# Units of every tile read from x1 in SBUF instead of through a copy in DRAM

## What is computed

```python
e = stack([tbl_f[ids[:, f]] for f in range(24)], axis=1)          # (1024, 24, 16)
Xk = e
for W in (W0, W1, W2):                                             # 64 outputs each
    Wr = W.reshape(24, Xk.shape[1], 64)
    Xk = einsum('bfd,bhd,fho->bod', e, Xk, Wr)
    outs.append(Xk.sum(axis=2))
z = concatenate(outs, axis=1)                                      # (1024, 192)
h = relu(concatenate([z, dense_ctx], axis=1) @ W_top1 + b_top1)    # 512
h = relu(h @ W_top2 + b_top2)                                      # 256
y = h @ W_top3
```

## Time and profile before

| | us |
|---|---|
| median of 3 runs | 585.45 |
| lowest and highest | 584.02 and 591.72 |
| the profiled execution | 578.03 |
| its span in the profile | 576.2 |

### The profile page before, as it was taken

One profiled execution on the slowest core, in us unless ns is written; L12 is line 12 of the kernel. 1 busy time (PEld: TensorE's weight loads), 2 busy tenths in 40 slices (PEclk: granted clock), 3 DMA queues, 4 the chain that ended last, 5 costly groups with the idle time before them and its releaser, 6 DMA issues.

```text
span 576.2 us, 7709 instructions
## 1 busy us (share of the span) xinstructions
PE 370.3 (64%) x3000; PEld 168.8 (29%) x3000; DVE 307.3 (53%) x305; ACT 137.1 (24%) x282; POOL 187.3 (33%) x196
## 2 busy tenths in 40 slices
PE   0010200856088439726998269755999998999995
PEld 0010000212022115302452025212553553553554
DVE  1010001473278347643789348526799798798930
ACT  1000000001022113302333123303253353251253
POOL 6777773027506720672017700771000000000000
PEclk9999999977779759976999869777999999999999
DMA  6000100191436326721757246702756847848300
GB/s 163 6 7 7 7 7 4 41 252 29 98 107 150 86 60 190 211 57 40 190 165 188 45 123 186 197 7 63 227 160 173 222 139 195 221 140 208 90 1 1
DMA packets 28039, 64.30 MB, mean 112 GB/s; under 512 B 7311, under 2 KB 10823, under 8 KB 28012
## 3 DMA queue, kind: packets, MB, share of 16 engines
q1 hardware_dynamic: 21868, 62.35, 40.3%
q0 software_dynamic: 6144, 1.59, 3.0%
HBM read 53.86 MB, written 5.85 MB: 104 GB/s over the span
## 4 chain that ended last, share of the span: by engine, by line
another core or an unknown queue 33%; PE 24%; DMA 14%; DVE 11%; issue 8%; ACT 4%; POOL 4%; SPq 2%; DVEq 0%; ACTq 0%
PE acc L622 14%; DVE pairs L416 8%; DMA units<-x_dram 5%; DMA turned<-x_dram 5%; POOL emb L388 4%; PE spread L596 2%; DMA x_dram<-common 2%; PE misc L683 1%; ACT x0diag L489 1%; DVE z L421 1%; SPq L328 1%; ACT x0parts L476 1%; DVE rest L284 1%; DMA units<-x 1%
## 5 line engine op out<-in xcount | busy, mean ns | idle before, releaser
L416 DVE TENSOR_TENSOR pairs<-spread,units 128x1024 f32<-128x1024 f32 x192 | 225.9, 1218 | 118.3 <-remote 76.4
L388 POOL DMA_INDIRECT emb<-in_tbl,ids_sb x192 | 187.1, 975 | 203.2 <-DVE parts L288 143.6
L622 PE MATMUL acc<-pairs,w_sb 128*64 128x512 f32 x768 | 205.2, 642 | 4.4 <-DVE pairs L416 4.3
L596 PE MATMUL spread<-x0parts,sel 72*64 72x512 bf16 (+1 forms) x280 | 50.6, 450 | 116.9 <-ACT common L476 39.6
L622 PEld LDWEIGHTS acc<-pairs,w_sb 128*64 128x64 f32 x768 | 53.3, 146 | 76.0 <-issue 54.3
L416 DVE TENSOR_TENSOR pairs<-turned,common 120x1024 f32<-120x1024 f32 x42 | 51.1, 1220 | 24.6 <-DMA turned<-x_dram 24.6
L596 PEld LDWEIGHTS spread<-x0parts,sel 72*64 72x64 bf16 (+1 forms) x280 | 14.6, 121 | 159.3 <-ACT common L476 71.4
L643 PE MATMUL misc<-ident_b,parts 128*72 128x128 bf16 x120 | 11.7, 253 | 67.0 <-DVE parts L288 36.9
L622 PE MATMUL acc<-pairs,w 120*64 120x512 f32 x180 | 49.6, 636 | 2.4 <-DVE z L421 2.1
L416 DVE TENSOR_TENSOR pairs<-spread,common 120x1024 f32<-120x1024 f32 x6 | 7.3, 1223 | 68.9 <-remote 65.1
L476 ACT ACTIVATE x<-acc 128x512 f32<-128x512 f32 x31 | 18.7, 602 | 96.8 <-PE acc L622 80.2
(11 more groups left out here) (57 smaller groups left out, 192.6 us busy)
## 6 DMA issues: line engine op xcount, KB each, us to landing
units<-x_dram SPq DMA_DIRECT2D x56, 512.0 KB, 6.2
turned<-x_dram SPq DMA_DIRECT2D x42, 480.0 KB
units<-x SPq DMA_DIRECT2D x16, 256.0 KB, 5.1
x_dram<-x SPq DMA_DIRECT2D x28, 128.0 KB
emb<-in_tbl,ids_sb POOLq DMA_INDIRECT x192
x_dram<-common SPq DMA_DIRECT2D x14, 96.0 KB
x_dram<-common SPq DMA_DIRECT2D x14, 56.0 KB
w_sb<-in_w SPq DMA_DIRECT2D x2, 384.0 KB
```

Source lines behind the costliest of these rows:

```text
L388: pool.indirect_dma_start(out=e3[:, f, :], out_offset=None, in_=tables[f], in_offset=bass.IndirectOffsetOnAxis(ap=ids_sb[:, t, f:f + 1], a ...
L416: dve.tensor_tensor(pairs[buf][0:rows, :], source[0:rows, :], other[0:rows, h * HALF:(h + 1) * HALF], ALU.mult).then_inc(pairs_done, 1)
L596: last = pe.matmul(spread[ring][lo:hi, half * BLK:(half + 1) * BLK], sel[:, first + lo:first + hi], src[:, cols(h, half)], start=True, sto ...
L622: last = pe.matmul(acc[half * H:(half + 1) * H, :], w, pairs[buf][0:rows, half * BLK:(half + 1) * BLK], start=first, stop=final)
```

## The change

The DRAM copy of x1 goes, with `store_x1`, its semaphore and its waits. `load_units` now loads every tile as `first_units` loaded tile 0: two DMAs of 256 KB per j straight from `x1` in SBUF, after x1_done. SP's order becomes: units of (0, 0) and (0, 1); then for each t from 1 to 7 the x0 store and the three turned loads of (t, 0), the same of (t, 1), the units of (t, 0), the units of (t, 1). ACT's `x1_read` waits are taken out. DVE's wait for the units counts two DMAs per load. Nothing else of PE, DVE, ACT or POOL changes.

```diff
--- before.py
+++ after.py
@@ -182,7 +182,6 @@
             return spread[o // 2 % 2][:, o % 2 * BLK:(o % 2 + 1) * BLK]
 
         x0_dram = [nc.dram_tensor(f"x0_dram{h}", (X0_ROWS, HALF), F32).ap() for h in range(2)]
-        x1_dram = [nc.dram_tensor(f"x1_dram{h}", (H, HALF), F32).ap() for h in range(2)]
 
         spread = [ctx.enter_context(nc.psum_tensor(f"spread{s}", [P, HALF], F32)) for s in range(2)]
         acc2 = ctx.enter_context(nc.psum_tensor("acc2", [P, 2, BLK], F32))
@@ -205,7 +204,6 @@
         common_done = sem("common_done")
         x0_stored = sem("x0_stored")
         turned_in = [sem(f"turned_in{c}") for c in range(L1_CHUNKS)]
-        x1_stored = sem("x1_stored")
         units_in = [[[sem(f"units_in{s}_{h}_{j}") for j in range(UNIT_GROUPS)] for h in range(2)] for s in range(2)]
         pairs_done = sem("pairs_done")
         main_done = sem("main_done")
@@ -300,33 +298,18 @@
                              (bt1_sb[:, :], bt1), (bt2_sb[:, :], bt2), (dense[H:H + D, :], dense_t)):
                 sp.dma_start(dst, src).then_inc(mlp_in, 16)
 
-            def store_x1(t, h):
+            def load_units(t, h):
 
                 sp.wait_ge(x1_done, 2 * t + h + 1)
-                for half in range(2):
-                    sp.dma_start(x1_dram[h][:, half * BLK:(half + 1) * BLK], x1[half * H:(half + 1) * H, h, :])\
-                        .then_inc(x1_stored, 16)
-
-            def load_units(t, h, js):
-
-                sp.wait_ge(x1_stored, 64 * (t - 1) + 32 * (h + 1))
-                for j in js:
+                for j in range(UNIT_GROUPS):
                     if t >= 2:
 
                         last = MIDDLE.items.index(("L2", FIELD_GROUPS - 1, j, h))
                         sp.wait_ge(pairs_done, item(t - 2, last) + 1)
-                    rows = x1_dram[h][j:H:UNIT_GROUPS, :].rearrange("v (u c) -> v u c", u=1)
-                    sp.dma_start(units[t % 2][:, j, h * HALF:(h + 1) * HALF], rows.to_broadcast([UNITS, FIELDS, HALF]))\
-                        .then_inc(units_in[t % 2][h][j], 16)
-
-            def first_units(h):
-
-                sp.wait_ge(x1_done, h + 1)
-                for j in range(UNIT_GROUPS):
                     for half in range(2):
                         rows = x1[half * H + j:(half + 1) * H:UNIT_GROUPS, h, :].rearrange("v (u c) -> v u c", u=1)
-                        sp.dma_start(units[0][:, j, h * HALF + half * BLK:h * HALF + (half + 1) * BLK],
-                                     rows.to_broadcast([UNITS, FIELDS, BLK])).then_inc(units_in[0][h][j], 16)
+                        sp.dma_start(units[t % 2][:, j, h * HALF + half * BLK:h * HALF + (half + 1) * BLK],
+                                     rows.to_broadcast([UNITS, FIELDS, BLK])).then_inc(units_in[t % 2][h][j], 16)
 
             def store_x0(t, h):
 
@@ -349,28 +332,14 @@
                     steps[1] = [HALF, J_CHUNK]
                     sp.dma_start(turned[c][:, :], bass.AP(rows.tensor, rows.offset, steps)).then_inc(turned_in[c], 16)
 
-            for h in range(2):
-                first_units(h)
-            store_x0(1, 0)
-            load_turned(1, 0, range(L1_CHUNKS))
+            load_units(0, 0)
+            load_units(0, 1)
             for t in range(1, TILES):
-
-                store_x0(t, 1)
-                load_turned(t, 1, range(L1_CHUNKS))
-                store_x1(t, 0)
-                load_units(t, 0, range(UNIT_GROUPS))
-                store_x1(t, 1)
-                if t < TILES - 1:
-
-                    load_units(t, 1, (0,))
-                    store_x0(t + 1, 0)
-                    load_units(t, 1, (1,))
-                    load_turned(t + 1, 0, (0, 1))
-                    load_units(t, 1, (2,))
-                    load_turned(t + 1, 0, (2,))
-                    load_units(t, 1, (3,))
-                else:
-                    load_units(t, 1, range(UNIT_GROUPS))
+                for h in range(2):
+                    store_x0(t, h)
+                    load_turned(t, h, range(L1_CHUNKS))
+                for h in range(2):
+                    load_units(t, h)
 
             sp.wait_ge(misc_free, rounds(TILES - 1) + len(SIDE_LAST) + len(TAIL))
             sp.dma_start(out.rearrange("b o -> o b"), y[:, :]).then_inc(stored, 16)
@@ -456,7 +425,7 @@
                         dve.wait_ge(common_done, 2 * (i + 1) + h + 1)
                     if layer == "L2" and c == 0:
 
-                        dve.wait_ge(units_in[slot][h][j], (i - slot) * 8 + 16 * (2 - slot))
+                        dve.wait_ge(units_in[slot][h][j], (i - slot) * 16 + 32)
                     if layer == "L1":
 
                         dve.wait_ge(turned_in[c], 32 * i + 16 * (h + 1))
@@ -525,17 +494,8 @@
                 act.wait_ge(spread_ready, number + 1)
                 copy(common[:, h * HALF:(h + 1) * HALF], spread[buf][0:COMMON_ROWS, :]).then_inc(common_done, 1)
 
-            def x1_read(eng, tile, h):
-
-                if isinstance(tile, int) and tile == 1:
-                    for j in range(UNIT_GROUPS):
-                        eng.wait_ge(units_in[0][h][j], 32)
-                elif not isinstance(tile, int) or tile > 1:
-                    eng.wait_ge(x1_stored, 64 * (tile - 2) + 32 * (h + 1))
-
             def take_x1(last_item, tile, h, bank):
 
-                x1_read(act, tile, h)
 
                 act.wait_ge(main_done, last_item + 1)
                 copy(x1[:, h, :], bank[:, :]).then_inc(x1_done, 1)
```

## The result

The changed kernel takes 592.2 us, median of 20 runs (588.25 to 601.11), beside 585.15 us for the kernel before, median of 20 (578.68 to 593.72). The ratio is 1.015, 95% interval 1.0123 to 1.0177: 1.5% slower. The forecast was 581 us; the number is inside its range and inside "within 2%", but on the other side of zero.

The account below looks back on a forecast made before the run. The prediction took PE's own work as the bound where POOL is silent, and gather stalls elsewhere. Gains of 2.1 + 1.0 + 1.2 = 4.3 us, other terms 0, off the 585.45 us median gave 581 us; range 568 to 596.

Parts of the forecast that it names:

- PE bound with some 4 us back: Likeliest case: PE's idle at the starts of bodies 1, 6 and 7 shrinks, 4.3 us in all; chance 0.45.
- the store's round trip: x1 stored to DRAM before SP's unit loads: without it body 5's loads can start 4.1 us earlier.
- Loads of 256 KB cost nothing: Sixteen smaller unit loads per tile: some 2.5 us more SP issue per half, covered by PE's work, counted as nothing.
- Paid in series: Unit loads' fixed DMA cost paid one after the other: 16 us more a tile; the in-series rival, near 800 us, chance 0.01.
- The reorder doesn't cost: Units of (t, 1) ahead of the next x0 store and turned loads: DVE gains slack PE can't use, value 0.
- These stalls belong to the gathers, which the change leaves alone: DVE's 141.6 us of "remote" waits come with the gathers, so the change was taken not to affect them.
- The stalls grow: Rival: units come sooner, so stalls begin sooner, up to 4.1 us more in four gathers; about 597 us, chance 0.13.
- The gathers come forward: Rival: earlier turned loads let DVE split tiles sooner, ending gathers and stalls earlier, 10 us more; about 571 us, chance 0.2.
- theory A: From the experiments: VectorE's operands come sooner, gathers start earlier against PE's work, and more PE signals fall into them.

Follow-up runs that it names:

- the hold: Gathers from tile 3 on held until PE reaches the split's item: kernel before 431.55 us (0.9973); changed kernel 426.43 (0.9861), 423.63 (0.9823) and 425.02 (0.9709).
- each half: Kernel before with SP's plain order alone, x1 via DRAM: 582.66 us (1.0123); changed kernel in the old order, units from SBUF: 584.84 (1.0102).

## Why the prediction was wrong

**PE bound with some 4 us back.** Right, and right in place. In bodies 5 and 6 PE is busy for 41.47 of 41.90 and 40.77 of 41.20 us, no item waits for units at a body start, and PE follows at once. Item 12 and 16 of body 5, body 6's unit issues, its first items, and PE's second spread:

```profile
470.38 1.23 DVE L385 TENSOR_TENSOR pairs<-turned,common 120x1024 f32<-120x1024 f32 x1 [0.57 <-DMA turned<-x_dram]
...
475.61 1.22 DVE L385 TENSOR_TENSOR pairs<-turned,common 120x1024 f32<-120x1024 f32 x1
...
496.88 6.42 SPq L311 DMA_DIRECT2D units<-x  x8
...
497.43 4.62 DVE L385 TENSOR_TENSOR pairs<-spread,units 128x1024 f32<-128x1024 f32 x4 [1.36 <-issue]
...
502.32 0.62 PE L556 MATMUL spread<-x0parts,sel 72*64 72x512 bf16 x4 [0.40 <-ACT x0parts L445]
```

The spread that stood at 485.60 with 2.41 us of idle, 6.9 us into body 6, stands at 502.32, 4.9 us into it, with 0.40 left behind ACT's copy. That is 2.0 of the 2.1 us by which the copy's end lay ahead. Body 6 gives 2.3 us and body 7 1.3 (54.0 to 52.7), where I had 2.1 and 1.0. The 1.2 us at body 1 can't be found: its start falls into a gather, and PE, which before did the spread at 191.70, now stands still from 186.94 until 212.60, behind ACT's copy at 211.05 shown above and the next one at 211.54.

**Too small a term all the same.** I counted three body starts, as only those showed idle behind units in the trace. Without gathers five of six show it, and the six tiles give 9.4 us together, 7.95 in the median; on a chip without stalls it is 15 us. The 4.1 us that I took for the store's round trip are those of body 5's units, and body 5 is a start without idle. Ahead of body 6, which has the idle, the round trip took 472.97 - 466.13 = 6.8 us:

```profile
466.13 1.15 SPq L307 DMA_DIRECT2D x_dram<-x  x2
472.97 2.49 SPq L319 DMA_DIRECT2D units<-x_dram  x4
```

So it goes in the other traces of the DRAM source: in the kernel before without gathers the five starts with idle follow round trips of 5.7 to 6.7 us and the one without a trip of 4.0; with the hold, of bodies 2 to 6 the three with over 2 us of idle follow 5.8 to 7.5, the two others 4.0 and 4.4. What makes a trip long isn't shown. I also left out that PE's idle can take its clock down.

**Loads of 256 KB cost nothing.** Right. Eight issues take 6.42 us, where I had 6.1, and they end ahead of the next x0 store. A load lands after 3.9 us. The Trainium skill (DMA: Bandwidth & Descriptors, Anatomy of one DMA) has about 2.0 us fixed for each DMA; the section is on DMAs issued from GpSimd, and these are issued by SP. Paid in series that was to cost 16 us a tile, and the pair of kernels without gathers, 1.6 us a tile faster, shows that it isn't paid in series.

**The reorder doesn't cost.** Right in these two kernels, by the steps given. Item 16 of body 5 stood 22.5 us into the body with a wait of 1.91 and stands 20.1 us into it (475.61 - 455.55) without any. With DRAM as the source VectorE's waits would have grown (41.3 us above), the time hardly (435.72 beside 433.78 us).

**"These stalls belong to the gathers, which the change leaves alone".** This is the step that failed. The premise was right: 129.5 us go with the gathers. The conclusion was not: how long a gather stretch lasts is no constant of the gather. In the two traces four stretches with the same gathers went from 248.4 to 266.8 us. I had set "remote" near 140 on DVE and named over 10 us of movement as the sign that I am wrong; it moved by 32. The term that I had at 0 measures 18.3 us in bodies 1 to 3 of the two profiled executions; less the 3.3 us of the others, and with 0.2 ahead of body 1 (183.53 to 183.70), it makes the 15.1 us between them. By the medians it is smaller: 7.05 us lost in all and 3.3 gained behind the gathers make some 10 us. The change's two signs are beyond the scatter: 1.5% slower (1.0123 to 1.0177) with the gathers and their stalls, 7.95 us faster without six of the gathers.

**The rivals.** *The stalls grow* is what happened: 4.6 us for each of four stretches in the traces, some 2.6 by the medians, where it had up to 4.1 and decided from 1.1. Its condition, that a stall begins where SP's transfers end, is not shown by anything here. *The gathers come forward* fails by its own objection. The wait for turned loads is gone, but the split of body 5 stands only 0.9 us earlier in its body (26.15 us into it, 27.05 before): VectorE now waits for PE's spread instead. DVE can't be further ahead than PE allows, as I had written against it.

**What stays open.** That the change costs with the stalls of the gathers and gains without them is shown. That each half lengthens the gather stretches is seen in single executions only; of the medians, the order's is just clear of no change and the source's isn't. Why the stretches lengthen is not shown. The lead at the gather's start fits one stretch of four, stretch 1 shows 5 us that it doesn't explain, and the hold that would have tested theory A never met the stalls. That loads out of SBUF cost during a gather by some other path is untested. Nor do the traces show what makes the stalls. The traces of the four kernels with stalls hold 3791 to 4227 updates of semaphores (the signals between engines), those of the fourteen runs without stalls 6843 to 7389. So part of what is "remote" may be a signal of this core whose record is missing.

## What to carry to other kernels

A stall that is "somebody else's" isn't a constant: if the change moves what runs beside it, give it a term with both signs, and weigh it by its size (here 141.6 us against a gain of 4). Look in which stretches the profile can show the gain at all, and follow a round trip in every tile and not in one (here 6.8 us where the wait is, 4.1 where it isn't), so that you know how often its wait can come. One profiled execution per kernel can differ by more than the change: here some 8 of 15 us. And if a kernel's time rests on such stalls, time the change on more than one chip: this one is 1.5% slower where the stalls are and 3.3% faster on a chip without them.

## What the runs showed of the hardware

The same kernel takes 577.42 us on one chip and 431.78 to 433.78 on three others. The difference of some 145 us is about the size of VectorE's "remote" waits (141.6 us), which are gone on the others. Whether it is the chip or the hour isn't separated: the stalls were there in the first two sets of runs and in none of the four later ones. The stalls begin ahead of the first tile. While POOL issues the first gathers on the stalling chip, ACT's copies of what PE has long written stand 11.2 us apart in the changed kernel, and the same in the kernel before (67.89 and 79.09):

```profile
67.64 1.02 ACT L445 ACTIVATE common<-spread 120x1024 f32<-120x1024 f32 x1 [10.18 <-remote]
78.84 1.02 ACT L445 ACTIVATE common<-spread 120x1024 f32<-120x1024 f32 x1 [10.18 <-remote]
...
57.51 1.92 PE L556 MATMUL spread<-x0parts,sel 72*64 72x512 bf16 x8 [18.29 <-issue]
68.72 1.06 PE L556 MATMUL spread<-x0parts,sel 72*64 72x512 bf16 x4 [9.29 <-issue]
```

PE had ended eight spread matmuls by 57.51 + 1.92 = 59.43, and ACT's copy of their result starts at 67.64, 8 us later; PE itself follows that copy's end at 68.66 at once, at 68.72. At this place, what comes late is the word that PE is done, not that of ACT. In the changed kernel without stalls the same copy starts at 41.35, 1.1 us behind the start of its spreads at 40.24. Its gathers issue at the same pace (starts at 158.38, 159.63 and 160.88, and at 239.07, 240.32 and 241.57 on the stalling chip), and the "remote" waits of VectorE are gone. That a program's own DMA issues can go with such a difference between chips is what I had least expected. The second thing is the clock behind an idle of 2.73 us: half speed for the next 2 us, and 1.5 us of PE time in that tile; it doesn't follow every idle of over 2 us.
